# Edge tiles of half node chunks with one selecting product each, in a graph layer with attention

## The reference

```python
xl = (x @ Wl).reshape(n, H, D)
xr = (x @ Wr).reshape(n, H, D)
msg = xl[src] + xr[dst]
act = jnp.where(msg > 0, msg, NEG_SLOPE * msg)
e = jnp.einsum('ehd,hd->eh', act, att)
m = jax.ops.segment_max(e, dst, num_segments=n)
p = jnp.exp(e - m[dst])
denom = jax.ops.segment_sum(p, dst, num_segments=n)
alpha = p / (denom[dst] + 1e-16)
out = jax.ops.segment_sum(alpha[..., None] * xl[src], dst, num_segments=n)
```

## Time and profile before

| | us |
|---|---|
| median of 3 runs | 1142.97 |
| profiled execution, device time | 1143.06 |
| its span, first to last instruction | 1141.3 |
| PE busy | 991.9 (87%) |
| DVE busy | 908.7 (80%) |
| ACT busy | 615.1 (54%) |
| POOL busy | 393.3 (34%) |

### The profile page before, as it was taken

One profiled execution on the slowest core, in us unless ns is written; L12 is line 12 of the kernel. 1 busy time (PEld: TensorE's weight loads), 2 busy tenths in 40 slices (PEclk: granted clock), 3 DMA queues, 4 the chain that ended last, 5 costly groups with the idle time before them and its releaser, 6 DMA issues. The chain is left out here.

```text
span 1141.3 us, 16739 instructions
## 1 busy us (share of the span) xinstructions
PE 991.9 (87%) x5061; PEld 799.5 (70%) x5061; DVE 908.7 (80%) x1572; ACT 615.1 (54%) x1378; POOL 393.3 (34%) x399
## 2 busy tenths in 40 slices
PE   2697799999999999999856899999996889999834
PEld 1585798999999999999833677777773344444422
DVE  5875577888888888888886999999984598878892
ACT  3264455666667676767524676777782243234311
POOL 0212777777777777777200000000002000000000
PEclk9998999999999999999986999999997999999966
DMA  9254688899898998888444786888882444233212
GB/s 239 44 191 114 206 252 272 263 273 274 270 285 268 295 293 273 287 268 261 126 144 167 220 247 219 246 252 266 235 247 56 127 111 104 72 78 82 44 31 36
DMA packets 108014, 220.79 MB, mean 193 GB/s; under 512 B 24350, under 2 KB 56695, under 8 KB 107819
## 3 DMA queue, kind: packets, MB, share of 16 engines
q1 hardware_dynamic: 86411, 153.91, 41.5%
q0 software_dynamic: 20064, 56.35, 21.5%
q10 hardware_dynamic: 1456, 9.46, 2.5%
HBM read 157.22 MB, written 73.01 MB: 202 GB/s over the span
## 5 line engine op out<-in xcount | busy, mean ns | idle before, releaser
L983 POOL DMA_INDIRECT score_gath<-xl_rows,misc x324 | 342.6, 1057 | 103.2 <-issue 96.3
L1023 PE MATMUL score_ps_m<-x_hi,score_w_hi 128*128 128x416 f32 (+1 forms) x576 | 209.8, 364 | 1.8 <-DVE score_w_lo L1176 1.7
L1024 PE MATMUL score_ps_m<-x_lo,score_w_hi 128*128 128x416 f32 (+1 forms) x576 | 204.8, 355 | 0.0
L1025 PE MATMUL score_ps_m<-x_hi,score_w_lo 128*128 128x416 f32 (+1 forms) x576 | 204.3, 355 | 0.0
L1652 PE MATMUL agg_ps_o<-agg_gath,agg_hot 128*125 128x256 f32 x648 | 184.2, 420 | 15.5 <-DVE agg_hot L1767 14.9
L1711 ACT ACTIVATE agg_gath<-agg_gath,prob 128x64 f32<-128x64 f32 x648 | 158.8, 337 | 4.9 <-DMA agg_gath<-edge_rows 4.3
L1155 DVE TENSOR_TENSOR score_zb<-score_gath,score_ps_x 128x1024 f32<-128x1024 f32 x81 | 98.8, 1220 | 74.9 <-PE score_ps_x L1006 65.3
L1652 PEld LDWEIGHTS agg_ps_o<-agg_gath,agg_hot 128*125 128x125 f32 x648 | 99.1, 190 | 50.2 <-issue 42.7
L1654 PE MATMUL agg_ps_o<-ext,agg_hot 128*125 128x18 f32 x324 | 117.8, 364 | 0.0
L1023 PEld LDWEIGHTS score_ps_m<-x_hi,score_w_hi 128*128 128x128 f32 x576 | 109.8, 191 | 3.9 <-issue 2.1
L1024 PEld LDWEIGHTS score_ps_m<-x_lo,score_w_hi 128*128 128x128 f32 x576 | 110.1, 191 | 1.1
(11 more groups left out here) (323 smaller groups left out, 1690.7 us busy)
## 6 DMA issues: line engine op xcount, KB each, us to landing
edge_rows<-score_gath SPq DMA_DIRECT2D x81, 520.0 KB, 4.0
agg_gath<-edge_rows SPq DMA_DIRECT2D x81, 520.0 KB, 4.9
local_bc<-local_rows SPq DMA_DIRECT2D x40, 224.0 KB
score_gath<-xl_rows,misc POOLq DMA_INDIRECT x324
xb_rows<-in_x ACTq DMA_DIRECT2D x1, 5000.0 KB, 17.6
phi_c<-phi_rows SPq DMA_DIRECT2D x10, 500.0 KB, 4.0
xb_rows<-in_L_mix_bo POOLq DMA_DIRECT2D x10, 500.0 KB, 7.0
x_bo<-xb_rows SPq DMA_DIRECT2D x10, 500.0 KB
```

The lines of the kernel that those rows point to most:

```text
L983: nc.gpsimd.indirect_dma_start(out=gath[:, g % GS, q, :], out_offset=None, in_=xl_rows, in_offset=bass.IndirectOffsetOnAxis(ap=src_idx[:, ...
L1023: pe.matmul(acc, w_hi[:, i % 2, kk, :], x_hi[:, kk, cols], start=(kk == 0), stop=False)
L1024: pe.matmul(acc, w_hi[:, i % 2, kk, :], x_lo[:, kk, cols], start=False, stop=False)
L1025: mm = pe.matmul(acc, w_lo[:, i % 2, kk, :], x_hi[:, kk, cols], start=False, stop=(kk == KC - 1))
```

## The change

The nodes are cut into twenty half chunks (`NS`), of 64 and 61 rows in turn. A half chunk's 64 high parts and its 64 low parts now fill the 128 partitions of `xr_parts`, and the selecting matrix is one at two partitions for each edge, so that one product gives the sum of both. Pairs are made of tiles and half chunks: 313 + 19, 332 in all, or 83 groups. The row numbers are stored and broadcast as bytes, four groups to a load (`LB = 4`), in one DMA to all 128 partitions, and the load for the next four groups stands ahead of `keep(g)` at the third group of a block.

```diff
-NPAIR = -(-(NT + NC - 1) // GP) * GP
+NS, HALF = 2 * NC, 64
+START = [C * (i // 2) + HALF * (i % 2) for i in range(NS)]
+NPAIR = -(-(NT + NS - 1) // GP) * GP
...
-LB = 2
+LB = 4
...
-    for part in ROWS_SPLIT:
-        sp.dma_start(k.local_bc[part, b % 2, 0:groups, :].rearrange("p g t -> p (g t)"),
-                     flat[:, LB * b * GP * TE:(LB * b + groups) * GP * TE].to_broadcast([part.stop - part.start, groups * GP * TE])
-                     ).then_inc(k.s_loc[b % 2], 16)
+    sp.dma_start(k.local_bc[:, b % 2, 0:groups, :].rearrange("p g t -> p (g t)"),
+                 flat[:, LB * b * GP * TE:(LB * b + groups) * GP * TE].to_broadcast([P, groups * GP * TE])
+                 ).then_inc(k.s_loc[b % 2], 16)
...
-                    if g % LB == 0 and g // LB >= 2 and g < NG:
-                        local(g // LB)
+                    if g % LB == LB - 2 and g // LB >= 1 and g + 2 < NG:
+                        local(g // LB + 1)
...
-                        for part in range(2):
-                            m = pe.matmul(ps_x[:, u, q // 2, (q % 2) * HID:(q % 2 + 1) * HID],
-                                          mask_t[:, u, q * TE:(q + 1) * TE],
-                                          xr_flat[:, ds(cs[q] * (2 * HID) + part * HID, HID)],
-                                          start=(part == 0), stop=(part == 1))
+                        m = pe.matmul(ps_x[:, u, q // 2, (q % 2) * HID:(q % 2 + 1) * HID],
+                                      mask_t[:, u, q * TE:(q + 1) * TE], xr_flat[:, ds(cs[q] * HID, HID)], start=True, stop=True)
```

In `prepare` the rows have to be moved to their partitions. PE does that with four products a chunk against a shifted identity, ACT copies the result, and the counts are nineteen passes instead of nine, of which the last nine stand behind two other steps:

```diff
+                def half_rows(c):
+                    pe.wait_ge(s_parts, c + 1)
+                    if c:
+                        pe.wait_ge(s_tcp, c)
+                    else:
+                        pe.wait_ge(s_tile, 1)
+                    for h in range(2):
+                        for i in range(2):
+                            at = HALF * (1 - i)
+                            t = pe.matmul(ps_c[:, h * HID:(h + 1) * HID], k.shift[0:C, h, at:at + P], k.xr_both[:, i, :],
+                                          start=(i == 0), stop=(i == 1))
+                    t.then_inc(s_tm, 1)
...
-                    for lag, stage in ((0, transposes), (2, down), (3, xd_transposes), (4, left_right)):
+                for i in range(NC + 5):
+                    for lag, stage in ((0, transposes), (2, down), (3, xd_transposes), (5, half_rows), (4, left_right)):
...
-                    act.activation(xr_parts[:, c, 0, :], xr[:, c % 2, :], ACT.Copy).then_inc(s_hi, 1)
+                    if c:
+                        act.wait_ge(s_tm, c)
+                    act.activation(k.xr_both[:, 0, :], xr[:, c % 2, :], ACT.Copy).then_inc(s_hi, 1)
+
+                def copy_halves(c):
+                    act.wait_ge(s_tm, c + 1)
+                    act.activation(xr_parts[:, 2 * c:2 * c + 2, :].rearrange("p s w -> p (s w)"), ps_c[:, 0:2 * HID], ACT.Copy
+                                   ).then_inc(s_tcp, 1)
...
+                count(0, NC)
                 low_part(2)
                 rms_scale(1)
+                count(NC, NS - 1)
+                v.sem_inc(s_cnt, 1)
                 v.wait_ge(s_cntp, 1)
```

More of the change, by code:

```diff
@@ L47 @@
 EARLY = [KC, 3, 3, 3, 3] + [0] * (NC - 5)
-assert NC * C == N and NJ * PERJ + 1 == NG and NPAIR <= PB * P
+assert NC * C == N and NJ == 8 and NPAIR <= PB * P
 class Tensors:
@@ L258, in prepare @@
         scratch = S("scratch", [C, EC])
-        counts = S("counts", [C, NC - 1])
-        bounds = S("bounds", [P, 2, NC - 1])
+        counts = S("counts", [C, NS - 1])
+        bounds = S("bounds", [P, 2, NS - 1])
         pair_iota = S("pair_iota", [P, PB])
         chunk_of = S("chunk_of", [P, PB])
-        chunk_125 = S("chunk_125", [P, PB])
-        cmp9 = S("cmp9", [P, NC - 1])
-        nine = S("nine", [P, NC - 1])
+        first_of = S("first_of", [P, PB])
+        chunk_c = S("chunk_c", [P, PB])
+        odd = S("odd", [P, PB])
+        place = S("place", [P, PB])
+        size_of = S("size_of", [P, PB])
+        cmp9 = S("cmp9", [P, NS - 1])
+        nine = S("nine", [P, NS - 1])
+        iota_64 = S("iota_64", [P, 1])
         tile_of = S("tile_of", [P, PB])
         tile_i = S("tile_i", [P, PB], I32)
-        chunk_i = S("chunk_i", [P, PB], I32)
+        chunk_i = S("chunk_i", [P, 2 * PB], I32)
         rows_d = S("rows_d", [P, PB, TE], I32)
@@ L344, in prepare @@
         s_lst = sem("s_lst", ctx)
+        s_tm = sem("s_tm", ctx)
+        s_tcp = sem("s_tcp", ctx)
         s_crow = sem("s_crow", ctx)
@@ L488, in chunk_counts @@
                     pe.wait_ge(s_cnt, 1)
-                    pe.matmul(ps_c[:, 0:NC - 1], ones[0:C, :], counts[:, :], start=True, stop=True).then_inc(s_cntp, 1)
+                    pe.matmul(ps_c[:, 0:NS - 1], ones[0:C, :], counts[:, :], start=True, stop=True).then_inc(s_cntp, 1)
                 def transposes(c):
@@ L628, in _ @@
                 normalise(4)
-                for i in range(2, NC + 4):
+                for i in range(2, NC + 5):
                     if i == 4:
@@ L639, in _ @@
                         act.dma_start(flat(k.xb_rows), flat(a["x"])).then_inc(k.s_xb, 16)
-                    for lag, stage in ((0, copy_xt), (2, copy_xd), (3, copy_xdt), (4, copy_lr)):
+                    for lag, stage in ((0, copy_xt), (2, copy_xd), (3, copy_xdt), (4, copy_lr), (5, copy_halves)):
                         if 0 <= i - lag < NC + (stage is copy_xdt):
@@ L779, in _, with count @@
                 rms_scale(0)
-                for c in range(NC - 1):
-                    q.do(v.tensor_scalar(scratch[:, :], o.dst_f[:, :], float(C * (c + 1)), None, ALU.is_lt, ALU.add,
-                                         accum_out=counts[:, c:c + 1]))
-                v.sem_inc(s_cnt, 1)
+                def count(first, end):
+                    for i in range(first, end):
+                        q.do(v.tensor_scalar(scratch[:, :], o.dst_f[:, :], float(START[i + 1]), None, ALU.is_lt, ALU.add,
+                                             accum_out=counts[:, i:i + 1]))
+                count(0, NC)
                 low_part(2)
                 rms_scale(1)
+                count(NC, NS - 1)
+                v.sem_inc(s_cnt, 1)
                 v.wait_ge(s_cntp, 1)
-                v.wait_ge(s_const, 6)
-                q.do(v.tensor_scalar(bounds[:, 0, :], ps_c[:, 0:NC - 1], 1.0 / TE, 63.5 / TE, ALU.mult, ALU.subtract))
+                v.wait_ge(s_const, 12)
+                q.do(v.tensor_scalar(bounds[:, 0, :], ps_c[:, 0:NS - 1], 1.0 / TE, 63.5 / TE, ALU.mult, ALU.subtract))
                 q.do(v.tensor_scalar(bounds[:, 1, :], bounds[:, 0, :], 12582912.0, 12582912.0, ALU.add, ALU.subtract))
```

103 lines of the change are left out of this document (65 added, 38 removed).

## The result

The changed kernel takes **1158.86 us** (median of 4 runs, 1158.5 to 1162.55) and the kernel before, beside it on the same chip, 1144.81. The ratio of the changed to the kernel before is **1.0148**, 95% interval 1.012 to 1.0176: slower, and by less than 2%. (One of the four runs of the kernel before took 2908.77 us; it is in the median and not in the ratio.) The forecast was 1156.

A forecast was written before the change was run, and what follows sets the result against it. POOL's gathers, at 5.47 us a group just below PE's 5.68, were taken as the next bound of `score`. 1143.06 + 13.7 (`prepare`) - 5.1 (`score`) + 4.3 (`aggregate`) = 1156 us; own range 1145 to 1166, 8 in 10 1134 to 1172.

The forecast's parts named there:

- POOL is the next bound: In `score`, POOL's gathers at 5.47 us a group limit the stage, so PE's 37.9 us saving yields only 5.1.
- Holds by operations with two SBUF operands: In `score`, gathers starting inside DVE operations with both operands in SBUF are held, adding 0.47 us a group.
- Score -5.1: `score` lasts 453.5 + 1.94 + 6.5 = 462.0 us against 467.1 before, 5.1 us less.
- `prepare`, first part: Ten more DVE counts 5.3 us, small operations 1.4 and PE's sum some 0.3: 7.0 us more.
- `prepare`, second part: New PE products add 3.5 us; waits for POOL's subtraction plus products in the last two iterations add 3.2.
- The tenth shift costs nothing: At the end of `prepare`, the tenth shift lies beside DVE's last table and adds no time.
- Row numbers give nothing: In `score`, ACT's 40.8 us of waits for row-number loads all go, without gain beyond the other terms.
- `aggregate` +4.3: Two more groups at the end of `aggregate`, where PE is the bound: 8 x 0.54 = 4.3 us more.
- 3: Rival, chance 0.05: in `score`, POOL is not the bound, gathers unheld at 5.0 us a group; 1117 us.
- 4: Rival, chance 0.11: `prepare` hides its additions, only 3.5 of 13.7 us remain; 1146 us.
- 1: Rival, chance 0.14: fewer gather holds in `score`, most groups taking 5.19 us; 1133 us.
- 2: Rival, chance 0.12: all groups in `score` held late, at 5.69 us a group; 1174 us.

The follow-up runs named there:

- reordering: Changed kernel with PE's `left_right` of chunk i - 4 put ahead of `half_rows` of chunk i - 5 in each `prepare` iteration; 1155.6 us, 1.0112.
- all four edits: Changed kernel with multiplication and phi each reading one PSUM operand, weight tiles loaded three groups earlier, `left_right` before `half_rows`; 1255.76 us (1.0231) and 1129.54 us (0.9878).

## Why the prediction was right, and where it was off

- **POOL is the next bound, so 38 us of products give 5.** Right, and shown from both sides: one gather less gives 36 us, four products more cost 4, each by one trace. The pace of 5.47 us a group came out exactly. No large errors cancelled in the sum: `prepare` was 1.0 us over it, `score` 2.1 over, `aggregate` 0.4 under, and the stage behind it, at which the sum had put nothing, took 0.4 more.
- **Holds by operations with two SBUF operands.** Right: no hold is left where an operand comes from PSUM. Of the gathers that start inside the multiplication 59 of 81 are held when it reads both operands from SBUF, and 0 of 75 when it reads one from PSUM; inside phi it is 13 of 15, and 0 of 30 and 0 of 20 in the two kernels where phi too reads one from PSUM. Why they are held was not shown.
- **Score -5.1.** It was -3.0. The gathers took the 453.5 us of the sum; the 2.1 us lie behind them. The last add is 3.59 us behind the last gather and not 1.94: the step that failed is that the gathered group is what is late next. The search behind POOL stopped at the gathered rows and did not look at SP, whose order ties DVE's weight tiles to gathers two groups ahead, nor at PE, for which the add before the last waits (1.08 us at 576.73). And from the last add to the last operation are 7.00 us and not 6.5: the `phi` that was to fall away is still there, at 582.43. With the tie to SP removed the stage took 462.2 us for the 462.0 of the sum, but that is in part luck: the gathers were 0.7 us shorter (452.8), and the two terms behind them 0.4 and 0.5 longer.
- **`prepare`, first part +7.0.** Measured +6.96 at the transposes of chunk 5. Leaving nine counts out gave 4.6 us at the same place, with the sooner start taken off, for the 4.8 that nine steps of 0.53 make.
- **`prepare`, second part +6.7.** Measured +7.7. The waits behind `half_rows` are real: reordering gave 2.6 us back (1.9 without the sooner start), where the sum had 2.2 for them without the products. "The tenth shift costs nothing" is doubtful: PE's last shift starts at 121.65 after 2.00 us of waiting, ACT's copy of it ends at 123.02, and DVE's last table at 122.98. They end together.
- **Row numbers give nothing.** The 40.8 us of waits vanished from ACT, and the gathers, which set the stage, kept their pace. No run takes this part of the change alone. The pass over bytes takes 0.71 us (median), that over bf16 took 0.72.
- **`aggregate` +4.3.** Measured +3.9. The copy of the sums is at 878.91 us, before 863.44, with `score` ending 11.6 later.
- **Rivals.** 3 (POOL not the bound) and 4 (`prepare` hides) fell to the runs above. 1 and 2, fewer or only late holds, did not occur, but the spread of 36.1 to 42.4 us says that the phase is a real, if smaller, source of difference.

## What to carry to other kernels

Before taking work from the busiest engine, work out the pace of the next one including its per-instruction gap; here "77% busy" was full. If POOL issues gathers beside DVE, give DVE's large operations an operand in PSUM, but only once POOL is the bound: the same edit was worth 0 and 18 us. And before moving work within an engine's order, ask which queue waits for its result with something urgent behind it, as POOL's list gathers had.

## What the runs showed of the hardware that was not expected

- A gather is held if it starts between about 0.02 and 1.0 us into a DVE operation of 1.22 us with two operands in SBUF; it then ends 0.82 us behind it, whether it is a `tensor_tensor` with a product, one with a difference, or phi's `scalar_tensor_tensor`. One that starts with the operation, to 0.01 us, is not held.
- With PE no longer full, its granted clock fell in stretches. In the changed kernel PE had 34.17 us of work in the 40 from 325 to 365, at a mean of 0.91; with one gather less it had 40.00 and 1.00 there, and everywhere from 205 to 525 us. In the changed kernel PE stood idle for 5.83 us, until 356.71, waiting for DVE's subtraction; the clock was 1.00 in the 10 us up to 355, 0.57 from 355 to 363, and in the 6 us from 356 to 362 it was 0.50. So part of what PE gained in slack went into a lower clock. What that cost wasn't separated; POOL's pace stayed 1.367 us a gather. What makes the clock fall was not tested. From the changed kernel, the stretch of 40 us, the three shorter ones, and PE's first product behind the wait:

```profile
325.00:365.00 40.00, 34.17 (x183) 33.30 (x182) 32.31 (x43) 25.25 (x39) 31.00 (x30) 0.91 0.84 259
...
345.00:355.00 10.00, 5.88 (x36) 5.64 (x35) 4.56 (x7) 3.93 (x7) 7.57 (x8) 1.00 0.95 276
355.00:363.00 8.00, 6.29 (x21) 6.08 (x22) 7.70 (x13) 3.92 (x8) 6.11 (x6) 0.57 0.84 298
356.00:362.00 6.00, 5.29 (x17) 5.12 (x18) 5.73 (x8) 3.61 (x6) 4.48 (x6) 0.50 0.80 270
...
356.71 0.69 PE L1078 MATMUL score_ps_m<-x_hi,score_w_hi 128*128 128x418 f32 x1 [5.83 <-DVE score_w_lo L1231]
```
- Two chips differ: the same kernel, that of all four edits, took 1255.76 and 1129.54 us, and its ratio to the kernel before was 1.0231 and 0.9878. A comparison from one chip doesn't hold for the other.
